# Attention scores formed transposed for 512 queries at a time, without transposes of probabilities, experts amid the attention steps

## What is computed

```python
s = einsum('bni,oi->bno', xn, W_spin) + b_spin
mean_field = mean(s, axis=1, keepdims=True)
global_influence = einsum('bmd,od->bmo', mean_field, W_global)
energy_fields = einsum('bnd,od->bno', s, W_J)
scores = einsum('bnd,bmd->bnm', energy_fields, s) / sqrt(128)
attn = tanh(beta * (s + global_influence + softmax(scores) @ s))

logits = xt @ Wg.T + bg                      # 16 experts, top 2 of them
gu = einsum('th,ehf->tef', xt, Wgu) + bgu    # gate = even columns, up = odd
glu = min(gate, 7) * sigmoid(1.702 * gate)
gated = (clip(up, -7, 7) + 1) * glu
ffn = sum over the top 2 of share * (gated @ Wd + bd)

out = x + attn + ffn
```

## Time and profile before

| | |
|---|---|
| median of 3 runs (lowest, highest) | 489.07 us (488.68, 489.25) |
| span of the profiled execution, first to last instruction | 486.7 us |
| instructions | 8984 |
| mean granted TensorE clock over the span | 0.943 |
| prologue, to PE's first scores | 42.4 us |
| attention of batch 0 and s of batch 1, to the experts' first product | 42.4 to 235.7 us |
| experts, first to last product | 235.7 to 344.2 us |
| attention of batch 1, and end | 344 to 486.7 us |

### The profile page before, as it was taken

How to read it: one execution, slowest core, us unless ns; L and a number is a source line. 1 busy time by engine, 2 the same in 40 slices (tenths; PEclk the granted TensorE clock), 3 DMA queues, 4 the chain that set the end, 5 groups by cost and what they waited for, 6 DMA issues and landing times. The chain is left out here.

```text
span 486.7 us, 8984 instructions
## 1 busy us (share of the span) xinstructions
PE 413.5 (85%) x2754; PEld 366.0 (75%) x2755; DVE 339.6 (70%) x728; ACT 249.2 (51%) x568; POOL 215.6 (44%) x222
## 2 busy tenths in 40 slices
PE   1879687795999998755699999999799999999980
PEld 1678576784878887644688898899688898888970
DVE  4696779699899695234366656656469888988863
ACT  5631664462655766133143443443577657766640
POOL 6000031745168777776132222222330655777772
PEclk9999899898999999857699999999899999999996
DMA  5990000000011111121314334332310221223221
GB/s 160 336 382 24 1 1 1 23 3 20 12 44 54 60 60 55 65 66 61 101 44 111 106 86 109 107 86 67 98 34 1 73 71 52 70 82 81 63 75 43
DMA packets 42061, 36.32 MB, mean 75 GB/s; under 512 B 4194, under 2 KB 38450, under 8 KB 42034
## 3 DMA queue, kind: packets, MB, share of 16 engines
q1 hardware_dynamic: 37940, 27.61, 18.7%
q0 software_dynamic: 4096, 8.40, 6.1%
HBM read 18.11 MB, written 17.87 MB: 74 GB/s over the span
## 5 line engine op out<-in xcount | busy, mean ns | idle before, releaser
L970 DVE TENSOR_TENSOR pTl<-T,pTh 128x512 fp32r<-128x512 f32 x180 | 122.1, 685 | 76.9 <-ACT pTh L741 76.7
L741 ACT ACTIVATE pTh<-T 128x512 fp32r<-128x512 f32 x180 | 108.4, 602 | 108.5 <-PE T L538 55.4
L538 PE MATMUL T<-ident,prob 128*128 128x128 f32 x512 | 81.4, 283 | 22.3 <-DVE pTl L970 12.8
L812 ACT ACTIVATE prob<-S,nmax 128x512 f32<-128x512 f32 x128 | 87.7, 691 | 17.8 <-DVE nmax L1167 17.7
L1163 DVE TENSOR_REDUCE mx<-S 128x1 f32<-128x512 f32 x128 | 85.0, 683 | 14.3 <-PE S L446 14.2
L538 PEld LDWEIGHTS T<-ident,prob 128*128 128x128 f32 x512 | 62.4, 145 | 42.0 <-DVE pTl L970 20.2
L444 PE MATMUL O<-pTh,sh 128*128 128x256 f32 x256 | 74.1, 289 | 0.2 <-ACT gb L884 0.2
L446 PE MATMUL O<-pTh,sl 128*128 128x256 f32 x256 | 73.3, 286 | 0.0
L445 PE MATMUL O<-pTl,sh 128*128 128x256 f32 x256 | 73.2, 286 | 0.0
L394 POOL DMA_INDIRECT slots_x<-xn,posu x64 | 62.8, 982 | 21.0 <-issue 18.4
L418 POOL DMA_INDIRECT xy<-slots_y,posu x64 | 60.8, 950 | 18.4 <-issue 17.7
(11 more groups left out here) (203 smaller groups left out, 832.3 us busy)
## 6 DMA issues: line engine op xcount, KB each, us to landing
slots_x<-xb SPq DMA_DIRECT2D x1, 5120.0 KB, 22.7
xy<-slots_x SPq DMA_DIRECT2D x20, 256.0 KB, 2.9
slots_y<-xy SPq DMA_DIRECT2D x20, 256.0 KB, 2.4
xn<-in_L_attn_x SPq DMA_DIRECT2D x8, 256.0 KB, 4.7
wl<-in_L_ffn_Wgu SPq DMA_DIRECT2D x1, 2048.0 KB, 14.4
xb<-in_L_attn_x SPq DMA_DIRECT2D x15, 128.0 KB, 2.4
part<-xb SPq DMA_DIRECT2D x8, 128.0 KB
slots_x<-xn,posu POOLq DMA_INDIRECT x64
```

Of the source, the lines that this page charges most:

```text
L538: m = nc.tensor.transpose(T[:, j % 2, a * P:(a + 1) * P], prob[:, half, (4 * j + a) * P:(4 * j + a + 1) * P], ident[:])
L741: nc.scalar.activation(dst, T[:, parity].rearrange("p (a b) -> p a b", a=4), ACT.Copy).then_inc(t_hi, 1)
L812: nc.scalar.activation(prob[:, half, 512 * j:512 * j + 512], S[:, j], ACT.Exp, bias=nmax[:, half:half + 1], accum_out=dn2[:, bass.ds(4 * q ...
L970: v.tensor_tensor(dst, T[:, parity].rearrange("p (a b) -> p a b", a=4), high.bitcast(F32), ALU.subtract).then_inc(t_lo, 1)
```

## The change

The file is written anew; what counts of it is this.

**Steps.** There are 8 blocks of 512 queries (4 a batch) and 16 key tiles in each: 128 steps. In a step PE forms the scores of one key tile (rows) against 512 queries (columns), ACT takes the exponential in place in PSUM and copies its high part, DVE takes the low part, and two steps later PE multiplies them by the key tile's xn (`values`). Nothing is transposed. Scores come out of xn alone: the weights are folded, `H = (spin weights) x (spin and J weights)`, and a block's `queries` are H xn.

**Feature 0.** Since a normalised token's features sum to zero, feature 0 is given by the others. Its place in xn holds the constant 1, and the weights are folded to match. So biases are in the products, and the values' product yields the row sum in feature 0. The queries' feature 0 holds the negated maximum. For it, PE forms one more product per 128 queries and 512 keys, of high parts alone (`maxima`, 16 a block), in the block before, DVE reduces them, `shift_row` turns the four columns, and `shift_in` writes the row.

**Banks.** Three PSUM banks for the scores, one for small products, two for the maxima, two for the result.

**Experts.** They stand after step 79 (`MOE_AT = 80`). The gate and up bias is in feature 0 of the weights, so its product goes; the down bias keeps it. Batch 1's spin products run in steps 18 to 25 and not in a stage of their own. Routing stands on DVE in 15 pieces in steps 29 to 54 (`ROUTE_AT`).

**POOL.** It normalises batch 1, folds and cuts the weights, scatters, and gathers, in this order; the batch-1 rows' low parts (`rows_lo`) stand behind the eighth scatter. Their high parts are made by ACT in steps 61 to 64, since their tile lies over the routing's.

```diff
-            def turn_prob(q, half, n, j):
-                t_free(n + j)
-                pe.wait_ge(exp_done, 4 * q + j + 1)
-                for a in range(4):
-                    m = nc.tensor.transpose(T[:, j % 2, a * P:(a + 1) * P],
-                                            prob[:, half, (4 * j + a) * P:(4 * j + a + 1) * P], ident[:])
-                m.then_inc(t_fill, 1)
...
-                    m = three(O[:, 0:2 * P], sh[:, t], sl[:, t], pTh[:, t], pTl[:, t], start=t == 0, stop=t == TB - 1)
...
+    LAG = 2
+    RING = 4
+    MOE_AT = 5 * TB
...
+            def maxima(k, q, a, c):
+                o = mx_bank(k, q)
+                if q == 0:
+                    pe.wait_ge(s_hi, s_no["G", k] + 1)
+                mm(o, gq[:, k % 3, 0, a * P:(a + 1) * P], xT[k // CB][:, 0, 512 * c:512 * c + 512],
+                   start=True, stop=True).then_inc(mx_fill, 1)
...
+            def score(i):
+                k, j = divmod(i, TB)
+                b = k // CB
+                o = s_bank("X", i)
+                if j == 0:
+                    pe.wait_ge(cr_done, k + 1)
...
+                three(o, xT[b][:, 0, j * P:(j + 1) * P], xT[b][:, 1, j * P:(j + 1) * P],
+                      gq[:, k % 3, 0], gq[:, k % 3, 1]).then_inc(s_fill, 1)
...
+                pe.wait_ge(s_lo, s_no["X", i] + 1)
+                m = three(O[:, k % 2], rows[b][:, 0, j], rows[b][:, 1, j], ph[:, i % RING], pl[:, i % RING],
+                          start=j == 0, stop=j == TB - 1)
+                m.then_inc(pv_done, 1)
...
+            def exponent(i):
+                n = s_no["X", i]
+                act.wait_ge(s_fill, n + 1)
+                A(S[:, n % 3], S[:, n % 3], ACT.Exp).then_inc(exp_done, 1)
...
+                act.wait_ge(exp_done, i + 1)
+                A(ph[:, i % RING], S[:, n % 3], ACT.Copy).then_inc(s_hi, 1)
...
+                if 61 <= i < 65:
+                    if i == 61:
+                        act.wait_ge(route_done, 1)
+                    c = i - 61
+                    A(rows[1][:, 0, 4 * c:4 * c + 4], xn[:, TB + 4 * c:TB + 4 * c + 4], ACT.Copy).then_inc(row_h[1], 1)
...
+            for c in range(2):
+                pool.wait_ge(routed, c + 1)
+                for t in range(NT):
+                    pool.indirect_dma_start(slots_x, bass.IndirectOffsetOnAxis(ap=posu[:, c, t:t + 1], axis=0),
+                                            xn[:, t], None).then_inc(scat, 16)
+                    if c == 0 and t == 7:
+
+                        pool.wait_ge(route_done, 1)
+                        for k in range(CB, NCH):
+                            pool.wait_ge(row_h[1], k - CB + 1)
+                            rows_lo(k)
...
+            for k in range(NSB):
+                if k >= 2:
+                    pool.wait_ge(base_ready, k - 1)
+                for t in range(4):
+                    for c in range(2):
+                        pool.indirect_dma_start(gy[:, k % 2, t, c], None, slots_y,
...
+                if k >= 1:
+                    fin(k - 1)
+            fin(NSB - 1)
...
+            WEIGH_AT = {MOE_AT + 8 + 6 * k + c: (k, c) for k in range(7) for c in range(2)}
```

More of the change, by code:

```diff
@@ L76, in sb, with over @@
             return ctx.enter_context(nc.sbuf_tensor(name, shape, dt))
-        def ps(name, shape):
-            return ctx.enter_context(nc.psum_tensor(name, shape, F32))
+        def over(*groups):
+            for group in groups[:-1]:
+                with ExitStack() as turn:
+                    yield [turn.enter_context(nc.sbuf_tensor(*t)) for t in group]
+            yield [sb(*t) for t in groups[-1]]
         def sem(name):
@@ new lines, in build, with field_at, query_at @@
+        SPIN_AT = {i: (0, i - 1) for i in range(1, 9)} | {i: (1, i - 18) for i in range(18, 26)}
+        GLOBAL_AT = {10: 0, 27: 1}
+        COUNT_AT = {39: 0, 45: 1}
+        def field_at(i):
+            k, r = divmod(i - 20, TB)
+            return (k, r // 2) if k >= 0 and r in (0, 2) and k not in (4, 7) else None
+        def query_at(i):
+            return i // TB + 2 if i % TB == 12 and i // TB + 2 < NSB else None
+        s_order = [("T", 0), ("T", 1), ("G", 0), ("T", 2), ("T", 3), ("G", 1)]
@@ L495, in _ @@
[L495 to L510 removed]
+                mm(o, ah, bh, start=start, stop=False)
@@ new lines, in step @@
+            def step(i):
+                k, j = divmod(i, TB)
+                score(i)
+                if i in TURN_AT:
+                    turn_tokens(TURN_AT[i])
+                if query_at(i):
+                    queries(query_at(i))
+                if k + 1 < NSB:
+                    for q in maxima_at(j):
+                        maxima(k + 1, q, q // 4, q % 4)
+                    if j == 13:
+                        shift_row(k + 1)
+                if i >= LAG and not MOE_AT <= i < MOE_AT + LAG:
+                    values(i - LAG)
+                if i in SPIN_AT:
+                    spins_and_logits(*SPIN_AT[i])
+                if i in GLOBAL_AT:
+                    global_row(GLOBAL_AT[i])
+                if i in COUNT_AT:
+                    count_pairs(COUNT_AT[i])
+                if field_at(i):
+                    fields(*field_at(i))
@@ L904, in rows_hi @@
+            shift_in(0)
+            for i in range(MOE_AT):
+                step(i)
+            values_hi(4)
             def rows_hi(n, bank, g, u):
@@ L948, in _ @@
             y_copy(NG - 2, 0, 16 * (NG // 2 - 1))
-            gated_hi(T_MOE + 2 * NG - 1, 1, NG - 1, 1)
+            gated_hi(2 * NG - 1, 1, NG - 1, 1)
             y_copy(NG - 1, 1, 16 * (NG // 2 - 1))
-            attention(1)
+            for i in range(MOE_AT, STEPS):
+                step(i)
+            values_hi(7)
+            squash(7)
         @block.vector
@@ L1133, in slots @@
[L1133 to L1138 removed]
+            tokens_lo(1)
+            inverse(3)
+            queries_lo(0)
+            for a in range(4):
+                maximum(0, a, a, 0)
+            for a in range(4):
+                maximum(0, 4 + a, a, 1)
```

1486 lines of the change are left out of this document (651 added, 835 removed).

## The result

The changed kernel took 507.13 us (median of 4 runs, 505.52 to 510.78), the kernel before 488.90 beside it: a ratio of 1.037 [1.033, 1.041]. The forecast was 471.8 us, with a range of 454 to 488. Both the sign and the range were wrong.

The account below looks back on a forecast made before the run. PE was taken to set the pace, DVE during routing. Step 64 at 183 us, last scatter 258, step 80 at 364.4, then 93 of gathers and 12 of tail: 469.4 span, plus 2.4, 471.8 us; range 454 to 488.

Parts of the forecast that it names:

- The wait: After step 79, PE stands 50 us for the slots, because 56 scatters queue behind batch 1's high parts.
- The routing: Steps 29 to 54: DVE is the bound with 61 us of work against PE's 48; 62 us.
- Experts ... 98 us: First to last experts' product: 108.5 us, less 2.7 of scores and 9.6 of bias products, plus 1 and 1.
- Steps 0 to 28: Batch 0 steps before routing: 40.9 steps, 7.5 maxima, 11.5 spin products, 5 turns, queries and fields; 65 us.
- 30 us without a wait: Prologue: DVE's moments, maxima, low parts and small pieces, with ACT's `shift_in` behind batch 1's moments.
- opening chain: Prologue: 7 us added for weights turned and folded and one query block; first score at 37 us.
- the scatters' descriptors: Rival at POOL's 56 scatters: DVE's two-port operations slow descriptor writes, 56 us more, 528 us; chance 0.02.
- dear exponential: Rival on ACT, every step: exponential in PSUM costs 1.3 us instead of 0.69, end at 499 us; chance 0.08.
- Handoffs cost more: Rival in the steps: handoffs over 3%, steps of 1.85 us, step 64 at 194, end at 483; chance 0.13.
- The 17 us: Whole kernel: forecast gain over the kernel before, 3.5%; faster was given 0.88.

Follow-up runs that it names:

- e2: Changed kernel plus 80 overwritten 256-column products where the gate and up bias products had been; 509.70 us, ratio 1.040 to the kernel before.
- e9: Changed kernel with two DVE operations swapped: gated product ahead of the low part of the next slots' rows; 492.87 us, ratio 1.007 to the kernel before.
- e1: Changed kernel with the register loads of `down` moved ahead of the turn of the gated value; 496.11 us, ratio 1.011 to the kernel before.
- e4: Changed kernel with the down biases' low part moved on DVE from step 5 to before step 0; 501.27 us, ratio 1.025 to the kernel before.
- t3: Changed kernel with ACT's first `shift_in` ahead of the deviations of batch 1; 504.38 us, ratio 1.024 to the kernel before.
- t2: Changed kernel with gated product first, batch 1's low parts on DVE, biases' low part before step 0, `shift_in` before deviations; 462.21 us, ratio 0.944.
- t1: Changed kernel with batch 1's low parts on DVE and the biases' low part before step 0; 481.41 us, ratio 0.981 to the kernel before.

## Why the prediction was wrong

- **What held.** The wait was found, placed and sized: PE stood 50.3 us (50 forecast), scatters at 1.26 us in portions of 8 and 56, last scatter 75.6 us after step 64 (75). From step 80 to the end it took 104.7 us (105.0), paced by gathers. The routing cost 58.5 us (62). These are the large terms, and they were read from rows.
- **What failed: "Experts ... 98 us".** The step said "Out of it go ... 4 bias products of 256 columns a group, 20 x 4 x 0.12 = 9.6 us". It priced a removed product at its busy time and did not ask whether PE waits next. PE's waits of 3.3 us for `gu_sb` in the kernel before were the sign that the chain ended just there. Measured, the stage took 120.9 us: the products were worth nothing (e2), the waits at L608 and L617 are 17.5 us where the kernel before waited 3.3 at the turn, and e9, which shortens the chain, takes the stage to 103.0.
- **The stage is even 12.5 us longer than before.** Removed work that is worth nothing leaves a stage as long as it was. What made it longer is a term that the forecast put at nothing: the second list of columns that `down` loads, four values more a group, behind a turn for which PE had drained. That part of a group went from 9.8 to 16.6 us over 16 groups, and to 6.5 in e1, which moves the loads. No run loads four values in the changed kernel. The window of the kernel before shows what else differs:

```profile
235.70:344.10 108.40, 104.07 (x804) 95.42 (x804) 65.50 (x104) 43.14 (x77) 25.68 (x20) 0.98 0.32 88
```

  Its clock is 0.98 against 0.90, and PE is busy 102.4 us with 718 products where it was busy 104.1 with 804. e2, with 0.97, is 3.1 us shorter over the 16 groups, so the clock may have cost about that much. What is left of the 12.5 us lies mostly at the stage's end (17.9 us for 16.9, though 2.7 us of scores had gone from there), and no run takes it apart.
- **Steps 0 to 28.** "Turns, queries and fields 5: 65 us" and the prologue's "30 us without a wait" had no stall in them. It was one DVE operation of 7.75 us, and steps at half clock behind it. e4 takes 5.9 us from the time. The prologue's 5.1 us were on no path by themselves (the trace of t3, and those of e4 and t2 side by side). Its 7 us for an opening chain "at the slow clock" rest on no row: the prologue's window gives a clock of 1.00, though its 512-column products stand 0.43 us apart and not 0.235. The Trainium skill, page "SBUF — State Buffer", section "SBUF: two separate sides", has a rule that covers this: a DVE operation with two SBUF inputs and a GpSimd operation that reads SBUF shut each other out, and whichever is later waits for the other's whole instruction. The traces agree on the exclusion (7.75 us). On the length they are of two kinds. `wglT` in t1 waited for the rest of one POOL operation. But for the biases' low part one instruction of 2.3 us would be at most the wait by that rule, and it was for the rest of four, issued back to back. I had cited this section for the scatters' descriptors, where it changed nothing, and not for POOL's weight sums.
- **The rivals.** A dear exponential fell: 128 of them in PSUM took 583 ns each, less than the 691 into SBUF. The Trainium skill, page "ScalarE: Activation LUTs", section "Step-by-step: what each stage is for", calls PSUM the faster destination. The figures agree with that but do not show it by themselves, since the bias and the row sums went from the exponential too, and no run tells the causes apart. From the page of the profile:

```profile
L724 ACT ACTIVATE PS<-PS 128x512 f32<-128x512 f32 x128 | 74.7, 583 | 74.1 <-PE PS L422 71.9
```

  "Handoffs cost more" had step 64 at 194, and it came at 192.8, but by a late first score and one stall. Steps 64 to 78 did take 1.81 us each (192.84 to 219.93), near this rival's 1.85 and over the 1.68 forecast; it cost nothing there, ahead of a wait of 50 us. The true rival, a ring in the experts that the shorter products expose, was not on the list. 
- **The sign.** The forecast put 0.88 on faster. The 17 us were the small difference of large terms (+30 at the scatters, -10 in the experts, -37 behind them). An error of 23 us in one stage was enough to turn it, and the range, 16 us upward, had no bound for the experts.

## What to carry to other kernels

Before a removed product is booked as a gain, look whether its engine waits in the same loop: if it does, even for 0.2 us, measure the chain from its start to that wait, and book only what the chain allows. Count register loads behind such a wait as work: four more values cost 0.4 to 0.5 us a group here. An order in which an operation that is waited for stands behind one that has more time is the cheapest thing to mend: two operations exchanged on DVE gave 14 us here. Where a wait is moved ahead of a long queue (56 scatters), the queue's whole length shifts with it, and a small operation taken over by another engine gave 17 us.

## What the hardware showed that I had not expected

- A DVE operation of 16x128 elements with two tiles of SBUF as inputs took 7.75, 8.56 and 9.24 us beside four operations of POOL, back to back, of 128x1024 elements with two such inputs. It ended with the last of them and not after one, of 2.3 us. Beside a single POOL operation, another DVE operation (`wglT`, 128x128) took up to 3.30 us in place of 0.30, and ended with it.
- Exposed register loads on PE's queue, eight values, cost 0.45 us a group, about as much as four 256-column products. From the turn ahead of them to the next product it was 1.11 us with eight values, 0.63 with four and 0.41 with none between.
- A wait costs twice: behind it PE's products of 512 columns stood 0.43 us apart in place of 0.23 for a while (64.91 to 67.04), which is the lower of the clock's two levels. The mean granted clock was 0.72 over 62 to 68 us, and 0.56 over 219.9 to 278.7, which holds the wait for the slots.
